# SwiGLU mixtures: each chunk's turned gates written to the board by one indirect DMA on GpSimd in place of four DMAs on SyncE

## The reference

```python
logits = jnp.einsum('bsd,de->bse', x, gate_w) + gate_b
probs = jax.nn.softmax(logits, axis=-1)
top_probs, top_idx = jax.lax.top_k(probs, 2)
top_probs = top_probs / jnp.sum(top_probs, axis=-1, keepdims=True)
dispatch = jnp.sum(jax.nn.one_hot(top_idx, n_experts, dtype=x.dtype) * top_probs[..., None], axis=-2)
h1 = jnp.einsum('bsd,edh->bseh', x, w1)
h2 = jnp.einsum('bsd,edh->bseh', x, w2)
hidden = jax.nn.silu(h1) * h2
expert_out = jnp.einsum('bseh,eho->bseo', hidden, w3)
return jnp.einsum('bseo,bse->bso', expert_out, dispatch)
```

## Time and profile before

| | |
|---|---|
| time, median of 2 runs | 1805.09 us (1803.96 to 1806.21) |
| span of the profiled execution | 1807.2 us |
| PE busy in the span | 1678.7 us (93%) |
| DVE, ACT, POOL busy | 1077.2, 966.8, 871.1 us |
| mean granted TensorE clock | 0.970 |
| steps of both SwiGLU mixtures | 128 us to 430 us, 1487 us to 1802 us of the span |
| DMAs that write turned gates, both mixtures | 56 of 16 KB, issued by SP |

### The profile page before, as it was taken

How to read it: one execution, slowest core, us unless ns; L and a number is a source line. 1 busy time by engine, 2 the same in 40 slices (tenths; PEclk the granted TensorE clock), 3 DMA queues, 4 the chain that set the end, 5 groups by cost and what they waited for, 6 DMA issues and landing times. The chain is left out here.

```text
span 1807.2 us, 32921 instructions
## 1 busy us (share of the span) xinstructions
PE 1678.7 (93%) x12503; PEld 955.4 (53%) x12503; DVE 1077.2 (60%) x1532; ACT 966.8 (53%) x1427; POOL 871.1 (48%) x730
## 2 busy tenths in 40 slices
PE   5879999999689999998999997999999769999998
PEld 3635555554244444444444445777777535555554
DVE  6667777766863332365334236666656467777766
ACT  2545555555236666526666645666666355555554
POOL 3318887877025333313333335333323008877777
PEclk8999999999799999998999998999999879999999
DMA  5004343333202222401222340000000004333333
GB/s 126 1 15 118 108 111 111 110 109 101 74 1 79 90 83 66 103 2 32 93 79 67 96 95 1 1 2 1 2 1 1 3 5 122 116 118 116 114 116 103
DMA packets 74948, 121.64 MB, mean 67 GB/s; under 512 B 18306, under 2 KB 22594, under 8 KB 74146
## 3 DMA queue, kind: packets, MB, share of 16 engines
q1 hardware_dynamic: 74786, 119.48, 22.7%
HBM read 115.74 MB, written 3.67 MB: 66 GB/s over the span
## 5 line engine op out<-in xcount | busy, mean ns | idle before, releaser
L766 POOL TENSOR_TENSOR x<-x,mx_gated 128x512 f32<-128x512 f32 x254 | 326.7, 1286 | 85.6 <-DVE mx_gated L718 83.4
L711 DVE TENSOR_TENSOR mx_hidden<-ps,mx_hidden 128x1024 f32<-128x1024 f32 (+1 forms) x256 | 246.2, 962 | 177.2 <-PE ps L579 176.7
L579 PE MATMUL ps<-tokens_high,w_high 64*128 64x512 f32 x1536 | 330.9, 427 | 8.7 <-ACT mx_hidden L873 5.0
L873 ACT ACTIVATE mx_hidden<-ps,w_bias 128x1024 f32<-128x1024 f32 x256 | 264.1, 1115 | 124.8 <-PE ps L579 124.8
L579 PE MATMUL ps<-tokens_high,w_low 64*128 64x512 f32 x1536 | 305.7, 393 | 0.0
L579 PE MATMUL ps<-tokens_low,w_high 64*128 64x512 f32 x1536 | 305.5, 393 | 0.0
L919 POOL TENSOR_TENSOR x<-x,mx_gated 128x512 f32<-128x512 f32 x126 | 161.5, 1282 | 253.3 <-DVE mx_gated L891 253.3
L891 DVE SCALAR_TENSOR_TENSOR mx_gated<-ps,w_bias,mx_gates 128x512 f32<-128x512 f32 x128 | 96.0, 750 | 280.1 <-PE ps L843 260.6
L694 ACT ACTIVATE mx_hidden<-ps 128x1024 f32<-128x1024 f32 x256 | 248.5, 1022 | 15.4 <-PE ps L579 1.4
L1884 DVE TENSOR_TENSOR c_near_weights<-c_near_hats 128x768 f32<-128x768 f32 x192 | 190.0, 1037 | 102.8 <-PE ps L1755 102.8
L648 PE MATMUL ps<-mx_hidden,w_second 128*64 128x512 f32 x1024 | 248.4, 605 | 0.4 <-DVE mx_hidden L711 0.4
(11 more groups left out here) (225 smaller groups left out, 1905.6 us busy)
## 6 DMA issues: line engine op xcount, KB each, us to landing
mx_gates<-gate_board SPq DMA_DIRECT2D x768, 128.0 KB, 3.1
w_first<-in_f_first SPq DMA_DIRECT2D x4, 1024.0 KB, 11.6
c_weight<-in_c_weight SPq DMA_DIRECT2D x1, 2304.0 KB
x<-in_x SPq DMA_DIRECT2D x8, 256.0 KB, 5.8
w_second<-in_f_second SPq DMA_DIRECT2D x4, 512.0 KB, 13.3
w_first<-in_f_first SPq DMA_DIRECT2D x4, 512.0 KB, 9.8
out_x<-x SPq DMA_DIRECT2D x16, 128.0 KB, 2.7
gate_board<-xn SPq DMA_DIRECT2D x56, 16.0 KB, 2.1
```

What stands on the lines that cost most here:

```text
L579: last = pe.matmul(out[h], weights[w][half(h), w_own], tokens[t][half(h), t_own], start=(p == 0), stop=(p == 2))
L711: dve.tensor_tensor(own, second[:, 0:halves, :], own, ALU.mult).then_inc(s.hidden.semaphore, 1)
L766: pool.tensor_tensor(place, place, gated[:, n % GATED, :], ALU.add).then_inc(s.added.semaphore, 1)
L873: act.activation(hidden[:, n % HIDDEN, f], first[:, (n * F + f) % BLOCKS], ACT.Gelu, bias=w.bias1[:, e * F + f:e * F + f + 1]).then_inc(s. ...
```

## The change

For the SwiGLU mixtures (`scattered`, where two halves by 16 experts fill the 32 partitions of a block) SP's four DMAs per chunk are gone. POOL issues one indirect DMA of 128 rows of 128 numbers instead, after add(n-2) in the pass for n = 16 i + 14, and waits for `s.rows` before it. A table of row numbers, `board_rows`, one column per chunk, tells where on the board each of the 128 rows goes; it is made on the host and loaded by one more DMA at the start. SP waits for the new semaphore `s.scattered` ahead of the first spread of each chunk but the first. The GELU mixtures keep their four DMAs. Chunk 0 is written as before. There are 7 indirect DMAs in each of the two mixtures, 14 in all, for 56 DMAs of SP.

```diff
     def posts(self, i):
-        return 16 * (1 + CHUNK_TILES * i)
+        return 16 * (1 + (0 if self.scattered else CHUNK_TILES) * i)
...
+    def scatter(self, pool, i):
+        self.s.rows.wait(pool, i + 1)
+        pool.indirect_dma_start(out=self.k.board.rearrange("r (c p) -> (r c) p", p=P),
+                                out_offset=bass.IndirectOffsetOnAxis(ap=self.k.board_rows[:, i:i + 1], axis=0),
+                                in_=self.k.xn[:, i * CHUNK:i * CHUNK + P],
+                                in_offset=None).then_inc(self.s.scattered.semaphore, 16)
+
     def spread_out(self, sp, n):
         i, e = n // self.E, n % self.E
         if e == 0:
-            self.s.posted.wait(sp, self.posts(i))
+            if i == 0 or not self.scattered:
+                self.s.posted.wait(sp, self.posts(i))
+            else:
+                self.s.scattered.wait(sp, 16 * i)
...
-            if e == post_at and i + 1 < CHUNKS:
+            if e == post_at and i + 1 < CHUNKS and not self.scattered:
                 self.post(sp, i + 1)
...
             if n >= 4:
                 add(n - 3)
             add(n - 2)
+            if n % E == TURN_AT + 5 and n // E + 1 < CHUNKS:
+                gates.scatter(pool, n // E + 1)
...
         k.loads = [(k.identity[:], ins["identity"], k.more_constants),
-                   (k.countdown[:], ins["countdown"], k.more_constants)]
+                   (k.countdown[:], ins["countdown"], k.more_constants),
+                   (k.board_rows[:], ins["board_rows"], k.more_constants)]
...
+    row, quarter = np.arange(P) % (P // 4), np.arange(P) // (P // 4)
+    c["board_rows"] = ((row * (N // P) + quarter)[:, None] + CHUNK_TILES * np.arange(CHUNKS)[None]).astype(np.int32)
```

More of the change, by code:

```diff
@@ L269, in _ @@
             if turn == 0:
-                pe.wait_ge(k.more_constants, 16 * 2)
+                pe.wait_ge(k.more_constants, 16 * 3)
         @block.scalar
@@ L484, in __init__ @@
         self.board = k.board[0:HALVES * E, :]
+        self.scattered = HALVES * E == P // 4
     def turn(self, pe, i, turned):
@@ L568, in count @@
             gate.base += 16 * HALVES * (steps // self.SLOTS)
+        if self.scattered:
+            s.scattered.base += 16 * (CHUNKS - 1)
         for signal, count in ((s.turned, CHUNKS), (s.rows, CHUNKS), (s.posted, self.posts(CHUNKS - 1)), (s.gated, steps),
@@ L2301, in __init__ @@
         self.posted = Counted(new("mx_posted"))
+        self.scattered = Counted(new("mx_scattered"))
         self.gate = [Counted(new(f"mx_gate{i}")) for i in range(Gates.SLOTS)]
@@ L2462, in build @@
         k.countdown = sb("countdown", [P, SWIGLU.experts])
+        k.board_rows = sb("board_rows", [P, CHUNKS], mybir.dt.int32)
         k.eps = {e: sb(f"eps{i}", [P, 1]) for i, e in enumerate((1e-5, 1e-6))}
```

## The result

The changed kernel takes 1821.3 us (median of 2 runs, 1820.5 to 1822.1) against 1805.1 us before: 1.0085 of it, with a 95% interval of 1.0055 to 1.0114. By the medians it is slower by 16.2 us, less than the 2% that were taken as the line.

What follows compares the result with a forecast made beforehand. PE was taken to bound the SwiGLU mixtures, busy 99.6 to 99.75 us of 100. Removing SP's writes gives 0, PE's stalls for POOL add 12.8 us to 1805.1: 1817.9 us, range 1804 to 1847.

Steps and rivals of the forecast that it cites:

- Nothing to gain on SP: SP's four writes, 1.98 us of its queue per chunk, are already hidden; removing them gives 0 us.
- The place of the cost: PE's third_layer of step 15 waits for POOL's multiplication behind the indirect DMA, at 14 chunk ends, longest at chunk 0.
- D: Time the indirect DMA holds POOL: 1.63 us, the middle of 1.98 (four SP issues) and 1.30 (light POOL instruction).
- 14 D - 10.1: PE's summed stalls at 14 chunk ends, 10.1 us being the free time in both mixtures; forecast 12.8 us.
- The free time at the ends of chunks 2 and 4: POOL's hold that costs PE nothing there: 0.44 us slack plus 0.23 us idle, 0.67 us.
- direct wait: PE's stall for POOL's multiplication of step 15; forecast 1.46, four of 0.75, two of 0.96 us per mixture.
- Nothing follows from it there: After PE's stall at a chunk end, POOL catches up within the next pair, with no further cost.
- Rival 4: Descriptor making waits for DVE's run at ends of chunks 0, 2, 4: 15 us more, 1833 us; chance 0.08.
- rival 3: Indirect DMA lands in 5 us, not 2.1, so DVE's gates come late: 27 us more, 1845; chance 0.1.
- rival 2: Slow descriptors, D from 3.2 us, and PE's clock falls after stalls: 1840 us, 1865 at D = 4; chance 0.15.

Runs made afterwards that it cites:

- pass_12_between: Changed kernel with the indirect DMA issued two steps earlier and between that pass's two POOL additions; 1.0013 of the kernel before.
- pass_12: Changed kernel with the indirect DMA issued two steps earlier, behind the additions of pass 12; 1.0025 of the kernel before.
- fenced: Changed kernel plus a small POOL memset behind each indirect DMA, on whose end POOL waits before multiplying; 1812.8 us, 1.0033 of the kernel before.
- direct_four: Changed kernel with four plain 32-row DMAs issued by POOL in place of the indirect DMA; 1830.8 us beside 1803.2 us, one run.

## Why the prediction was right, and where it was not

The forecast was 1818 us, the result 1821.3 us, within the range, and slower by 16.2 us where 12.8 were forecast.

- *Nothing to gain on SP* held. The four writes are gone, no gate operation waits less, and pass_12_between, which has the change almost without its costs, stands at 1.0013.
- *The place of the cost* held: the stretch of the third products behind the multiplication of step 15, at every chunk end, and longest at the end of chunk 0 (0.95 us).
- *D* was mis-sized: 1.63 us forecast, 1.19 measured. An indirect DMA of 128 rows is cheaper than four issues on SP (1.98 us). The estimate of 1 us from the Trainium skill, "DMA: Bandwidth & Descriptors", section "Latency and other measured facts", was nearer, though the page's figure is for the first byte, than the middle of the forecast's two rows. With D = 1.19 the sum 14 D - 10.1 gives 6.6 us.
- *The free time at the ends of chunks 2 and 4* was read too small. The forecast took the multiplication's 1.51 us there as given; in the changed kernel it takes 1.28 us, as DVE's operation of line 413 (248.10 to 248.53) is over before it starts and no longer delays it, so 0.67 us becomes some 0.9. The direct wait is therefore the same at all ends of chunks 1 to 6: the third products take 2.17 us at the end of chunk 2 and 2.19 at the end of chunk 5, each in place of 1.94. With 0.25 us for each of these twelve ends, and 0.95 and 0.86 us for chunk 0, the direct waits are 4.8 us, not 6.6. pass_12, where DVE is never held by more than one instruction of POOL, measures 4.9.
- *"Nothing follows from it there"* is the step that failed. The forecast let POOL catch up at no cost. The other 11.8 us, 16.6 less 4.8, are DVE's router operations, held behind POOL at 8 of 14 chunk ends, and PE's wait for DVE behind them. Fenced confirms the size: it has 9.4 us less, although its fence puts PE off by another 0.17 us an end, read at the ends of chunks 5 and 6 where DVE has no router operations (0.42 in place of 0.25). For 14 ends that is 2.4 us, and 9.4 + 2.4 = 11.8.
- *Rival 4* named the right pair of engines and the wrong direction. It let the indirect DMA wait for DVE, for 15 us at the ends of chunks 0, 2 and 4. In fact none of the 14 takes more than 1.15 us, and DVE waits for POOL, at the ends of chunks 1 to 4. The sentence taken there from the Trainium skill, "SBUF — State Buffer", that GpSimd can't write descriptors while DVE is in a 2-port mode, played no part; no run here shows such a hold. The Trainium skill, "SBUF — State Buffer", section "SBUF: two separate sides", also says that a DVE operation with two SBUF inputs and a GpSimd one that reads the SBUF shut each other out for a whole instruction. The rows agree as far as that goes: line 417 takes 0.18 us where no such POOL instruction runs (fenced) and 1.15 us beside one (before). The 3.08 us, a hold through more than one instruction, go beyond it.
- *The gates late* (rival 3): landing took 2.3 us, and DVE never waited for the spreads.
- *The clock* (rival 2) did not fall: the longest stall is 1.5 us, and the window over the end of chunk 1 keeps the granted clock at 1.00 (2.4 GHz). The row has the length, the busy us of PE, PEld, DVE, ACT and POOL, the granted clock, the DMA share and GB/s:

```profile
205.00:211.00 6.00, 5.36 (x34) 2.59 (x32) 5.70 (x6) 2.53 (x3) 4.79 (x4) 1.00 0.08 25
```

So the total was right within 4 us by luck: the direct waits were put too large by 8.0 us (12.8 for 4.8), and a term of 11.8 us was left out.

## What to carry to other kernels

An instruction put on a half-idle engine costs by what stands behind it in the queue and by its slack there; read both at the very place, and read the idle time that separates it from the next user of a shared resource. In this kernel a DMA issued by GpSimd did best ahead of an idle time of GpSimd, with no two-input VectorE operation before that idle time. Where it stood elsewhere, a fence between it and the next GpSimd instruction was cheaper (7.2 us) than letting that one run ahead (16.6 us). A DMA that nobody waits for gives nothing when it is taken away.

## What the runs showed of the hardware

- An indirect DMA of 512-byte rows from SBUF to DRAM holds GpSimd for 1.01 us with 128 rows and 0.90 us with 32, and GpSimd is idle for 0.15 us ahead of it. With 128 rows it lands 2.3 us after its issue in the changed kernel and 3.2 us in pass_12. A plain DMA of 32 such rows holds GpSimd for 0.50 us and lands in 1.6 us (direct_four).
- While GpSimd works on an indirect DMA, the instruction queued behind it already keeps DVE out, though its row in the profile begins later: with a fence between the two, DVE's operation took 0.18 us in the middle of the DMA, without one 3.08 us. The Trainium skill, "GPSIMD Engine Reference", section "Instruction dispatch", says that a core of GpSimd goes on to the next instruction as soon as its share of the last is done, and that consecutive instructions are no barrier; by the Trainium skill, "Perfetto Trace Analysis", section "DMA Instruction — SWDGE (GPSIMD)", two of GpSimd's cores make the descriptors. The traces agree with both, in that the fence took the hold away (3.08 to 0.18 us) and that an ordinary copy of 0.99 us in the DMA's place made no such hold. Which cores run ahead no profile here shows.
- The profile shows a DVE operation that is held out by POOL as busy. Of the 3.08 us of the operation on 16 numbers only 0.18 are its own by fenced, and no list of waits has the rest.
